# Node stages of a two-layer graph kernel: row statistics and normalising by chunks of seven tiles, and one subtraction moved from VectorE to GpSimd

## The reference

```python
def _layernorm(x, axis=-1, eps=1e-05):
    m = jnp.mean(x, axis=axis, keepdims=True)
    v = jnp.var(x, axis=axis, keepdims=True)
    return (x - m) / jnp.sqrt(v + eps)
...
    # attention of layer 0
    h = (x @ W.T).reshape(n, H, D)
    ...
    alpha = jnp.einsum('ehd,hd->eh', h_src, a_src) + jnp.einsum('ehd,hd->eh', h_dst, a_dst)
...
    # attention of layer 1
    h = (x @ W).reshape(n, HEADS, OUT_C)
    a1 = jnp.sum(h * attn_l, axis=-1)
    a2 = jnp.sum(h * attn_r, axis=-1)
...
    x = x + _L0_gnn_ref(_layernorm(x, axis=-1), ...)
    x = x + _L0_ffn_ref(_layernorm(x, axis=-1)[None], ...)[0]
    x = x + _L1_gnn_ref(_layernorm(x, axis=-1), ...)
    x = x + _L1_ffn_ref(_layernorm(x, axis=-1)[None], ...)[0]
```

## Time and profile before

| what | value |
|---|---|
| median of 3 runs | 6250.21 us (6245.75 to 6252.14) |
| the profiled execution's own time | 6253.11 us |
| its span in the trace | 6251.4 us |
| mean granted TensorE clock | 0.883 of full speed |
| PE busy, share of the span | 4504.6 us, 72% |
| DVE busy | 3544.0 us, 57% |
| ACT busy | 1454.2 us, 23% |
| POOL busy | 3674.1 us, 59% |
| node phase of layer 0, first DMA issue to the next phase's first | 127.69 to 236.14 us |
| node phase of layer 1, the same | 3430.02 to 3532.06 us |

### The profile page before, as it was taken

The page is one execution under the profiler, slowest core; times in us unless marked ns, Lnnn a source line. Parts: engine busy times, 40 slices in busy tenths (PEclk is TensorE's granted clock), DMA queues, the critical chain, the costliest instruction groups (busy, mean ns, idle before and its releaser), DMA issues. The chain is left out here.

```text
span 6251.4 us, 96537 instructions
## 1 busy us (share of the span) xinstructions
PE 4504.6 (72%) x19217; PEld 3440.8 (55%) x19217; DVE 3544.0 (57%) x6578; ACT 1454.2 (23%) x3118; POOL 3674.1 (59%) x3755
## 2 busy tenths in 40 slices
PE   0678888888888885699998446565565655664898
PEld 0345555555555554599998334354453444554898
DVE  6678888888888877521221335344454443547444
ACT  1333333333333323122222201011110110113222
POOL 1577777777777751133333277777777777741333
PEclk9899999999999995799999668788787887885999
DMA  7566666666666644366666555555555555535555
GB/s 227 183 164 167 168 169 167 167 168 169 165 168 169 165 118 153 106 179 185 184 179 187 128 134 144 140 139 143 136 143 141 138 143 137 142 91 168 185 195 190
DMA packets 705207, 991.04 MB, mean 159 GB/s; under 512 B 300534, under 2 KB 520890, under 8 KB 682865
## 3 DMA queue, kind: packets, MB, share of 16 engines
q0 software_dynamic: 184848, 489.78, 31.0%
q1 hardware_dynamic: 513468, 484.16, 25.8%
q10 hardware_dynamic: 6564, 14.14, 0.7%
HBM read 868.78 MB, written 121.43 MB: 158 GB/s over the span
## 5 line engine op out<-in xcount | busy, mean ns | idle before, releaser
L782 POOL DMA_INDIRECT e_rows<-sc_table,e_eidx x3224 | 3082.0, 956 | 1013.6 <-issue 926.5
L888 PE MATMUL e_ps_o<-e_rows,e_oh 128*128 128x264 f32 x6344 | 1619.7, 400 | 46.9 <-DVE e_rows L1172 32.9
L888 PEld LDWEIGHTS e_ps_o<-e_rows,e_oh 128*128 128x128 f32 x6344 | 1218.9, 197 | 339.1 <-issue 115.0
L1172 DVE TENSOR_TENSOR e_rows<-e_rows,e_ps_w 128x1024 f32<-128x1024 f32 x806 | 969.2, 1206 | 5.3 <-ACT e_rows L984 5.2
L991 ACT COPY e_res<-e_ps_o 32x264 f32<-32x264 f32 x793 | 291.0, 367 | 1864.7 <-PE e_ps_o L894 1454.3
L858 PE MATMUL e_ps_X<-e_ident,e_alog 128*104 128x128 f32 x496 | 96.1, 356 | 773.2 <-ACT e_alog L968 773.2
L1820 PE MATMUL x_ps_h<-x_xT,x_w 128*128 128x256 f32 x2624 | 647.0, 405 | 5.2 <-DMA x_b<-in_L_ffn_b_dram 5.2
L1820 PEld LDWEIGHTS x_ps_h<-x_xT,x_w 128*128 128x128 f32 x2624 | 637.9, 337 | 9.6 <-issue 5.9
L1831 PE MATMUL x_ps_y<-x_w,x_hT 128*128 128x256 f32 x2624 | 580.0, 380 | 0.0
L964 ACT ACTIVATE e_encr<-e_ps_enc 128x512 f32<-128x512 f32 x806 | 473.5, 591 | 397.8 <-PE e_ps_enc L817 383.1
L1831 PEld LDWEIGHTS x_ps_y<-x_w,x_hT 128*128 128x128 f32 x2624 | 494.5, 191 | 62.0
(11 more groups left out here) (332 smaller groups left out, 4677.1 us busy)
## 6 DMA issues: line engine op xcount, KB each, us to landing
x_w<-in_L_ffn_W_dram SPq DMA_DIRECT2D x112, 1024.0 KB
e_at<-sc_grp SPq DMA_DIRECT2D x403, 192.0 KB
x_w<-in_L_ffn_w_dram SPq DMA_DIRECT2D x60, 1024.0 KB
e_rows<-sc_table,e_eidx POOLq DMA_INDIRECT x3224
e_at<-sc_grp SPq DMA_DIRECT2D x403, 96.0 KB
sc_agg<-e_res SPq DMA_DIRECT2D x816, 33.0 KB
e_fr<-sc_rec SPq DMA_DIRECT2D x62, 312.2 KB
e_hp<-sc_hp SPq DMA_DIRECT2D x403, 48.0 KB
```

Source lines behind the costliest of these rows:

```text
L782: pool.indirect_dma_start(rows[:, k, s, j, :], None, dr["table"][:, :], bass.IndirectOffsetOnAxis(eidx[:, k, s, j:j + 1], 0)).then_inc(s_r ...
L888: nc.tensor.matmul(place, oh[:, k, at_j:at_j + P], rows[:, k, s, j, :], start=(j == 0), stop=False)
L1172: nc.vector.tensor_tensor(part, part, ps_w[:, k, :, s * HEADS:(s + 1) * HEADS].unsqueeze(3).to_broadcast([P, CH, HEADS, DH]), ALU.mult).th ...
```

## The change

In both node phases the statistics no longer stand ahead of everything. `stats(t)` is one `bn_stats`. `moments(c)` makes the variances of chunk c (four operations on 128x7 values), `roots(c)` on ACT their square roots, `factors(c)` means and reciprocals (three operations). DVE does chunk 0 whole, normalises three tiles, then does the statistics and moments of chunk 1. In the loop each iteration t gets the `bn_stats` of tile t + 14 (while there is one), iterations 6, 13, 20, 27 and 34 end with the moments of the chunk two ahead, and iterations 3, 10, ..., 38 begin with the factors of the next chunk. On ACT the square roots of chunk c + 1 stand at the head of iteration 7c. In layer 0 the subtraction that makes `hr` goes from DVE to POOL (`first_rest`), one tile ahead of POOL's other subtraction.

```diff
@@ block.gpsimd
             if first:
+                def first_rest(t):
+                    k = t % U
+                    pool.wait_ge(s_row, t + 1)
+                    pool.wait_ge(s_p0, t + 1)
+                    if t >= U:
+                        pool.wait_ge(s_p2, t - U + 1)
+                    nc.gpsimd.tensor_tensor(hr[:, k, :], row[:, k, 0:D], hp[:, k, 0, :], ALU.subtract).then_inc(s_r1, 1)
+
+                first_rest(0)
                 for t in range(NT):
                     k = t % U
+                    if t + 1 < NT:
+                        first_rest(t + 1)
                     pool.wait_ge(s_p1, t + 1)
                     nc.gpsimd.tensor_tensor(hp[:, k, 2, :], hr[:, k, :], hp[:, k, 1, :], ALU.subtract).then_inc(s_p2, 1)
@@ block.scalar
-            act.wait_ge(s_var, 1)
-            nc.scalar.activation(std[:, :], var[:, :], ACT.Sqrt, bias=eps[:, 0:1]).then_inc(s_std, 1)
+
+            def roots(c):
+                act.wait_ge(s_var, c + 1)
+                nc.scalar.activation(std[:, c * U:(c + 1) * U], var[:, c * U:(c + 1) * U], ACT.Sqrt, bias=eps[:, 0:1]).then_inc(s_std, 1)
...
+            roots(0)
             copy_x(0)
             copy_x(1)
             for t in range(NT):
+                if t % U == 0 and t + U < NT:
+                    roots(t // U + 1)
                 if t + 2 < NT:
                     copy_x(t + 2)
                 copy_h(t)
@@ block.vector
-            for c in range(U):
-                v.wait_ge(s_x[c], 32 if first and c == U - 1 else 16)
-                for t in range(c * U, (c + 1) * U):
-                    nc.vector.bn_stats(st[:, t, :], xs[:, t, :]).then_inc(s_stat, 1)
-            v.wait_ge(s_stat, NT)
-
-            done(nc.vector.tensor_tensor(mean[:, :], st[:, :, 1], st[:, :, 4], ALU.add))
...
+            def moments(c):
+                cs = slice(c * U, (c + 1) * U)
+                v.wait_ge(s_stat, U * (c + 1))
+                done(nc.vector.tensor_tensor(dif[:, cs], st[:, cs, 1], st[:, cs, 4], ALU.subtract))
+                done(nc.vector.scalar_tensor_tensor(dif[:, cs], dif[:, cs], 0.25, dif[:, cs], ALU.mult, ALU.mult))
+                done(nc.vector.tensor_tensor(var[:, cs], st[:, cs, 2], st[:, cs, 5], ALU.add))
+                done(nc.vector.scalar_tensor_tensor(var[:, cs], var[:, cs], 1.0 / D, dif[:, cs], ALU.mult, ALU.add))
+                v.sem_inc(s_var, 1)
+
+            def factors(c):
+                cs = slice(c * U, (c + 1) * U)
+                done(nc.vector.tensor_tensor(mean[:, cs], st[:, cs, 1], st[:, cs, 4], ALU.add))
+                done(nc.vector.tensor_scalar(mean[:, cs], mean[:, cs], 0.5, None, ALU.mult))
+                v.wait_ge(s_std, c + 1)
+                done(nc.vector.reciprocal(rstd[:, cs], std[:, cs]))
@@ parts(t)
-                v.wait_ge(s_row, t + 1)
-                v.wait_ge(s_p0, t + 1)
-                if t >= U:
-                    v.wait_ge(s_p2, t - U + 1)
-                nc.vector.tensor_tensor(hr[:, k, :], row[:, k, 0:D], hp[:, k, 0, :], ALU.subtract).then_inc(s_r1, 1)
                 v.wait_ge(s_r1, t + 1)
                 nc.vector.tensor_copy(hp[:, k, 1, :], hr[:, k, :]).then_inc(s_p1, 1)
@@ the order on DVE
+            for t in range(U):
+                stats(t)
+            moments(0)
+            factors(0)
             for t in range(3):
                 normalise(t)
+            for t in range(U, 2 * U):
+                stats(t)
+            moments(1)
             for t in range(NT):
+                c, k = divmod(t, U)
+                if k == 3 and c + 1 < U:
+                    factors(c + 1)
                 if t + 3 < NT:
                     normalise(t + 3)
+                if c + 2 < U:
+                    stats(t + 2 * U)
                 if first:
                     parts(t)
                 else:
                     logits(t)
+                if k == U - 1 and c + 2 < U:
+                    moments(c + 2)
```

## The result

| kernel | median us (runs) | against the kernel before |
|---|---|---|
| before | 6249.71 (6245.75 to 6253.24, 6 runs) | |
| changed | 6273.95 (6270.37 to 6277.6, 6 runs) | ratio 1.0039, 95% interval 1.0026 to 1.0052 |

A forecast was written before the change was run, and what follows sets the result against it. Layer 0's node loop was taken as paced by DVE, then by POOL after the change, layer 1's by PE; +4.3 us and -15 us gave -10.7, so 6239.5 us from 6250.2, range 6225 to 6253.

The forecast's parts named there:

- Any edge or expert stage whose length moved by more than 3 us, which nothing in the change should do.: Sign, outside the node phases, that would show the forecast wrong: a stage length moving over 3 us.
- The sum: Whole kernel: +4.3 us in layer 0 and -15 us in layer 1 make -10.7 us, giving 6239.5 us.
- What DVE no longer does is worth nothing, since POOL has become the bound: Layer 0's node loop: POOL sets the pace, so DVE's dropped subtraction saves nothing; layer 0 becomes 4.3 us slower.
- 1.55 us a tile: Layer 0's node loop: POOL's step, taken between 1.46 and 1.63, 76.0 us for 49 tiles; ends 1.40 and 1.70.
- 76.0 + 5.4: Layer 0's node loop: 76.0 us for 49 tiles, plus 5.4 for factors meeting a busy POOL, 0.9 six times.
- steady orders: Layer 0's node loop: two DVE-POOL orders, POOL running on at 1.46 us a tile, or the cast winning at 1.63.
- Roots, 2.3 us each: Layer 0's node loop, tiles 7c: POOL runs dry while ACT waits for moments, 2.3 us five times, 11.5 in all.
- The head: Before the node loops: first normalised tile 17.8 us earlier in layer 0 and 16.8 us earlier in layer 1.
- Layer 1: Node phase of layer 1: -16.5 + 1.5 = -15 us, between -12.5 and -15.5.
- second rival: Layer 1's node loop held by DVE at 1.3 us a tile: -9 us there, 6245 us total; chance 0.11.
- Who excludes whom: Layer 0's node loop: POOL's subtraction and DVE's subtraction, cast and normalising exclude each other; by the rule `bn_stats` goes free.
- third rival: Layer 0's node loop: every DVE operation, `bn_stats` too, excludes POOL's; 2.45 us for 35 tiles, +28, 6278 us; chance 0.07.

The follow-up runs named there:

- e1_shift38: Changed kernel plus 38 tiny memsets in VectorE's idle plan-phase time, putting layer 0's edge-loop head at 969: 6248.5 us, ratio 0.9995.
- e2_before218: Kernel before plus 218 such memsets in the same idle place, putting layer 0's edge-loop head at 1187: 6275.04 us, ratio 1.004.
- e8_hr_on_dve: Changed kernel with the `hr` subtraction back on VectorE and 196 memsets bringing the edge-loop head to 1225: 6228.38 us, ratio 0.997.
- e5_roots_later: Changed kernel with 38 memsets, ACT's square roots moved from the head of iteration 7c to 7c + 2: 6238.34 us, ratio 0.9984.

## Why the prediction was wrong, step by step

- **"Any edge or expert stage whose length moved by more than 3 us, which nothing in the change should do."** This step failed, and it decided the sign: +21 us in layer 0's edge phase. The sum put every phase but the two node phases at nothing, since "a node phase that ends earlier moves everything behind it by as much". The change did something to that phase after all, it moved its code by 38 places. No term, bound or rival stood for it, though the 4.1 us at each jump back were in the trace of before. `e1_shift38` takes the loss away with empty instructions, and `e2_before218` brings it on without the change.
- **"What DVE no longer does is worth nothing, since POOL has become the bound", and 1.55 us a tile.** POOL was busy for 64% of the loop. Nor had DVE been the bound before ("layer 0 is paced by DVE"): of its 65.5 busy us some 0.35 a tile were the subtraction being held (0.77 against 0.42 us), and in `e8_hr_on_dve` DVE does a `bn_stats` more per tile at the same step. What the change took from DVE was time in which it stood still. The step is a ring of two tiles: 1.66 us undisturbed, 1.89 in the mean with the factors and what stalls leave behind. The terms 76.0 + 5.4 = 81.4 us (49 tiles and the factors) measured 91.8, which is 100.7 less 8.9 for the roots. The two "steady orders" looked at the exclusion between DVE and POOL only, and not at who waits for the normalised tile.
- **Roots, 2.3 us each.** The mechanism was right and the size off: 1.8, five times. From the end of the `hr` ahead to the next one it was 156.57 - 153.82 = 2.75 us and not 3.1, and without the root POOL would have had its row at 0.98 and not at 0.8.
- **The head.** Right: 18.2 us earlier instead of 17.8 in layer 0, 16.5 instead of 16.8 in layer 1.
- **Layer 1.** -12.9 us instead of -15, near the end of -12.5 that was given: the rows take 3.2 us more where 1.5 were charged. Moving the roots gains 2.9 there (`e5_roots_later`), so the waits for roots were priced too low at 0.2 us each. The second rival (held by DVE, -9) did not come.
- **Who excludes whom.** Right: normalising, subtraction and cast are held by POOL's subtractions and `bn_stats` is not, so the third rival was near the measured time with its 6278 us by luck, and false in its mechanism.
- **The sum.** Without the second fetch the change is -1.1 us (`e1_shift38`), where -10.7 was forecast: 8 us from layer 0's loop and 2 from layer 1. That would have lain in the range, but with POOL wrongly taken for the bound.

## What to carry to other kernels

Count the instructions of every rolled loop, and where a loop is too long to stay loaded (519 waited at each jump here, 227 did not), expect a change of size anywhere ahead of it to move its time: compare with a few empty instructions put in an idle place before a small gain or loss is believed. Before an engine is called the bound, follow one tile round the loop through all engines and divide by the number of tiles in flight; one more tile of lead was worth 15 to 17 us here, and moving work off the "full" engine cost 13 to 16. Where a stretch of unchanged code has become longer, look at the granted clock too, turn by turn: part of the loss came with it here. Time that an instruction spends held by another engine counts as busy in the profile, and other work can stand in it for nothing.

## What was not expected of the hardware

- A jump back to the head of a loop of 519 DVE instructions cost some 4 us of idle time each turn. Where the head stood 38 places earlier a second wait of 1.8 to 3.1 us (2.2 in the mean) came in place of one of 0.56. A loop of 227 paid 0.3 us. The effect returned after 256 places, in both directions: edge phase of layer 0 at head 931 2165.2 us and at 1187 2167.2; at 969 2139.0 to 2144.0 and at 1225 2137.4 to 2143.3.
- TensorE's granted clock fell to 1.2 GHz at most jumps back, and every 3.4 us at that level went with a turn 1.0 to 1.6 us longer. With the head at 943 it also fell in the middle of the body in 4 of 12 turns, behind a wait of 0.45 us on DVE.
- DVE operations on 128x7 values took 0.58 to 0.66 us beside a running POOL subtraction, and 0.17 alone, so a chain of small operations is dear just where POOL is kept busy.
- Two POOL subtractions of 128x256 in a row start 0.63 us apart, though each is listed with 0.67: the step of 1.46 us that the forecast made of them with a gap of 0.06 each does not exist.
